# Gram matmuls of a tile in two bursts instead of four groups, and GpSimd's gathers tied more closely to TensorE, in a recommendation tower

## What is computed

```python
e = jnp.stack([tbl_0[ids[:, 0]], ..., tbl_26[ids[:, 26]]], axis=1)   # 2048 x 27 x 128
dot_products = jnp.einsum('bnd,bmd->bnm', e, e)
r, c = np.tril_indices(27, k=-1)
h = jnp.concatenate([dot_products[:, c, r], dense_ctx], axis=1)      # 2048 x 367
h = jnp.maximum(h @ W_top1 + b_top1, 0.0)                            # 512
h = jnp.maximum(h @ W_top2 + b_top2, 0.0)                            # 256
y = h @ W_top3                                                       # 1
```

## Time and profile before

| | us |
|---|---|
| three runs | 361.26, 360.29, 360.21 |
| median | 360.29 |
| profiled execution: span from the first to the last instruction | 358.7 |
| what lies around the span, by the median | 1.6 |
| TensorE busy, matmuls | 333.7 (93%) |
| VectorE busy | 246.3 (69%) |
| ScalarE busy | 144.4 (40%) |
| GpSimd busy | 250.4 (70%) |

### The profile page before, as it was taken

One profiled execution on the slowest core, in us unless ns is written; L12 is line 12 of the kernel. 1 busy time (PEld: TensorE's weight loads), 2 busy tenths in 40 slices (PEclk: granted clock), 3 DMA queues, 4 the chain that ended last, 5 costly groups with the idle time before them and its releaser, 6 DMA issues.

```text
span 358.7 us, 13616 instructions
## 1 busy us (share of the span) xinstructions
PE 333.7 (93%) x6094; PEld 303.4 (85%) x6094; DVE 246.3 (69%) x329; ACT 144.4 (40%) x265; POOL 250.4 (70%) x271
## 2 busy tenths in 40 slices
PE   1879699989999989999999999999999999999896
PEld 0779499978999979898889989999899989997775
DVE  3959979975488935878197965968387955961142
ACT  2536524444433433335343453435343353435320
POOL 5777777777777777777777777777777777777200
PEclk9969989999999999999999999999999999999999
DMA  6997744534333353443333452434533443322100
GB/s 184 306 318 196 205 136 107 102 93 91 83 93 82 90 99 75 96 96 80 93 88 82 115 85 77 105 84 81 102 89 83 99 98 74 84 55 55 27 3 1
DMA packets 26155, 36.86 MB, mean 103 GB/s; under 512 B 8451, under 2 KB 20099, under 8 KB 26098
## 3 DMA queue, kind: packets, MB, share of 16 engines
q0 software_dynamic: 8448, 17.32, 20.5%
q1 hardware_dynamic: 17506, 18.16, 20.1%
q10 hardware_dynamic: 144, 0.52, 0.4%
HBM read 35.97 MB, written 0.01 MB: 100 GB/s over the span
## 4 chain that ended last, share of the span: by engine, by line
PE 57%; POOL 26%; issue 10%; DVE 3%; DMA 3%; ACT 1%; DVEq 0%; ACTq 0%
POOL rows L450 26%; PE e_banks L482 25%; PE w_banks L543 9%; PE g_banks L513 8%; PE w_banks L554 7%; PE e_banks L494 6%; DMA rows<-in_tbl,idx 2%; DVE one_hot L672 2%; PE w_banks L532 1%; DVE zt L686 1%; DMA idx<-in_idx 1%; ACT et L340 0%; ACT h L333 0%; ACT et L350 0%; DVE a L720 0%
## 5 line engine op out<-in xcount | busy, mean ns | idle before, releaser
L450 POOL DMA_INDIRECT rows<-in_tbl,idx x264 | 249.6, 945 | 82.9 <-issue 78.0
L672 DVE TENSOR_TENSOR one_hot<-ids_wide,row_no 128x1024 fp32r<-128x1024 int32 x160 | 186.3, 1215 | 76.5 <-PE e_banks L482 72.5
L482 PE MATMUL e_banks<-one_hot,table_hi 128*128 128x256 f32 x672 | 172.2, 294 | 3.4 <-issue 3.4
L482 PE MATMUL e_banks<-one_hot,table_lo 128*128 128x256 f32 x672 | 167.0, 287 | 0.0
L482 PEld LDWEIGHTS e_banks<-one_hot,table_hi 128*128 128x128 f32 x672 | 131.4, 196 | 4.4 <-issue 4.2
L482 PEld LDWEIGHTS e_banks<-one_hot,table_lo 128*128 128x128 f32 x672 | 131.6, 196 | 0.2
L350 ACT ACTIVATE et<-e_banks 128x256 f32<-128x256 f32 x84 | 57.9, 689 | 89.3 <-PE e_banks L482 89.3
L340 ACT ACTIVATE et<-e_banks 128x512 f32<-128x512 f32 (+1 forms) x68 | 45.0, 664 | 52.3 <-PE e_banks L494 51.5
L513 PEld LDWEIGHTS g_banks<-et 128*26 128x26 f32 x4096 | 41.7, 103 | 17.7 <-issue 13.3
L513 PE MATMUL g_banks<-et 128*26 128x26 f32 x4096 | 50.0, 191 | 1.8 <-DVE zt L686 1.3
L494 PE MATMUL e_banks<-ident,rows 128*128 128x128 f32 x264 | 43.0, 285 | 5.5 <-DMA rows<-in_tbl,idx 5.5
(11 more groups left out here) (25 smaller groups left out, 67.7 us busy)
## 6 DMA issues: line engine op xcount, KB each, us to landing
ids_wide<-in_ids SPq DMA_DIRECT2D x80, 128.0 KB
et<-in_kept_tables SPq DMA_DIRECT2D x10, 512.0 KB, 10.1
rows<-in_tbl,idx POOLq DMA_INDIRECT x264
et<-in_kept_tables ACTq DMA_DIRECT2D x1, 512.0 KB, 3.9
a1T<-in_ids SPq DMA_DIRECT2D x4, 128.0 KB, 10.8
w<-in_w SPq DMA_DIRECT2D x2, 256.0 KB
w<-in_W_top SPq DMA_DIRECT2D x1, 512.0 KB
w<-in_w SPq DMA_DIRECT2D x1, 222.0 KB
```

Of the source, the lines that this page charges most:

```text
L450: pool.indirect_dma_start(rows[:, k % RING, a, :], None, tables[f], bass.IndirectOffsetOnAxis(ap=idx[:, t, f:f + 1], axis=0)).then_inc(row ...
L482: last = nc.tensor.matmul(e_bank[n % E_BANKS][:, 0:UNIT], part[:, q, c, :], one_hot[:, hot_slot(o, piece), c % PIECE, :], start=(c == 0 an ...
L672: nc.vector.tensor_tensor(one_hot[:, hot_slot(o, piece), :, :], ids_place(o).unsqueeze(1).broadcast_to([P, PIECE, UNIT]), row_no[:, piece ...
```

## The change

`BURST_AT` is new: the gram pieces 0 to 3 of a tile stand together at the end of the tile's first tick `at`, pieces 4 to 7 with `turn` and `pack` at the end of tick `at + 2`. `g_filled` is counted up after each burst, so VectorE waits for two. Gram pieces no longer alternate with turns of `h`; look-ups and layers do. The loads by which look-ups are placed are new. GpSimd waits, from chunk 4 on, for the transposes of chunk k - 4 (`AHEAD_BY = 3`), and for every burst that stands in tick k - 4 or earlier.

```diff
+AHEAD_BY = 3
...
+    HALF = G_PIECES // 2
+    BURST_AT = []
     for t in range(LAST_TILE):
         at = TILE_AT[t + 1] + (t == 0)
-        for p in range(G_PIECES):
-            step = [("G", t, p)] + ([("turn", t), ("pack", t)] if p == G_PIECES - 1 else [])
-            grams[at + p * 4 // G_PIECES].append(step)
+        for half, tick in enumerate((at, at + 2)):
+            grams[tick] += [("G", t, p) for p in range(half * HALF, (half + 1) * HALF)]
+            BURST_AT.append(tick)
+        grams[at + 2] += [("turn", t), ("pack", t)]
...
-    COLUMNS = {"T": 1024, "OH": 4096, "G": 1024, "H": 1024, "L1": 3072, "L2": 4096}
-    LOOK_UPS_FROM = [0, TILE_AT[1] + 1] + [TILE_AT[PAIR * (u - 1)] + 4 for u in range(2, UNITS + 1)]
-    load = [sum(COLUMNS[step[0][0]] for step in turns[k] + layers[k] + grams[k]) for k in range(TICKS)]
+    COLUMNS = {"T": 1024, "OH": 4608, "G": 768, "H": 768, "L1": 3072, "L2": 4096}
+    LOOK_UPS_FROM = [0, TILE_AT[1] + 1] + [TILE_AT[PAIR * (u - 1)] + 3 for u in range(2, UNITS)] + [TILE_AT[LAST_TILE]]
+    load = [COLUMNS["T"] + sum(COLUMNS[step[0]] for part in turns[k] + layers[k] + [grams[k][:HALF]] for step in part)
+            for k in range(TICKS)]
...
-        for step in look_ups[k] + layers[k]:
-            STEPS += step
-        for turn, piece in itertools.zip_longest(turns[k], grams[k], fillvalue=[]):
-            STEPS += turn + piece
+        for turn, step in itertools.zip_longest(turns[k], look_ups[k] + layers[k], fillvalue=[]):
+            STEPS += turn + step
+        STEPS += grams[k]
...
-                if k >= RING:
-                    pool.wait_ge(t_filled, k - RING + 1)
+                if k > AHEAD_BY:
+                    pool.wait_ge(t_filled, k - AHEAD_BY)
+                bursts = sum(tick <= k - AHEAD_BY - 1 for tick in BURST_AT)
+                if bursts:
+                    pool.wait_ge(g_filled, bursts)
...
-                if p == G_PIECES - 1:
+                if p % HALF == HALF - 1:
                     last.then_inc(g_filled, 1)
...
-                dve.wait_ge(g_filled, t + 1)
+                dve.wait_ge(g_filled, 2 * (t + 1))
```

## The result

| | before | changed |
|---|---|---|
| median of six runs | 360.45 | 363.93 |
| lowest and highest | 360.2 to 362.13 | 362.61 to 364.92 |
| ratio (95% interval) | | 1.0093 (1.0071 to 1.0114) |
| profiled execution: span | 358.7 | 361.6 (that run: 363.37) |
| TensorE busy | 333.7 | 334.0 |

The forecast was 359.8 us, in 358.7 to 362.0. The time lies outside, on the slow side.

What follows compares the result with a forecast made beforehand. GpSimd's gathers, one per 1.25 us, were taken as the bound. +0.4 at chunk 67's transposes and -0.9 in the tail gave -0.5 us on 360.29: 359.8 us, range 358.7 to 362.0.

Steps and rivals of the forecast that it cites:

- (1): Grams in bursts: each two pairs joined into four pieces save 0.22 us, 6.6 us of TensorE in all, hidden behind gathers.
- TensorE will arrive earlier: At chunks' transposes: TensorE, saved 6.6 us by bursts, reaches chunks that have not landed; only a few tenths gained at chunk 67.
- (3): GpSimd running three chunks ahead: its wait for chunk k-4's transposes bites nowhere, 3 us to spare at chunk 44; cost 0.
- (7): TensorE's clock: gaps of about 2 us before chunks 65 and 66 would not lower it before the tail; taken as 0.
- GpSimd decides at the end: Chunks 24 to 67: gathers need 207.5 us, TensorE 204.5, so GpSimd's 1.25 us cadence sets when the last chunk is in.
- (2): Look-ups placed anew: the same 84, lumps of two per tick covered by GpSimd's cadence; priced at nothing, bound 1.5 us a lump.
- (4): GpSimd's waits for bursts: chunk 10's gather starts 0.3 to 0.6 late, never made up; +0.5 us, bounds 0 and 1.0.
- (5): Tail: tile 14's last grams move ahead of chunk 67's transposes; tile 15's grams start 1.75 us after those, 0.9 less than before.
- (6): Start of chunk 67's transposes: last gather ends at 334.5, 2.0 us of landing, so 336.5 against 336.13, +0.4 us.
- B: Rival: GpSimd's new waits bite more often, as bursts save nothing or look-ups lump; three more stops, 361.3 us; chance 0.08.

Runs made afterwards that it cites:

- e5: The kernel before, gathering only chunks 0 to 6, with later chunks reading those rows again and nothing waiting for gathers: 355.82 us, 0.9878.
- e6: The changed kernel, gathering only chunks 0 to 6, later chunks reading those rows again, without GpSimd's waits: 352.17 us, 0.9794.
- e1: The changed kernel without GpSimd's wait for bursts, its wait for the transposes of chunk k-4 kept: 364.55 us, 1.0101.
- e4: The kernel before in its old order, with GpSimd's new waits for chunk k-4 and for gram groups: 361.89 us, 1.0055.
- e3: The kernel before with only the grams changed: two bursts of four instead of four groups of two, turns of h in a row ahead: 375.46 us, 1.0402.
- e2: The changed kernel with all of GpSimd's waits as before (seven chunks of room, no bursts): 364.74 us, 1.0101.
- e9: The changed kernel with SyncE's plain loads of the same bytes, from fixed places, replacing the gathers of chunks 7 to 67: 354.66 us, 0.9735.
- e10: The changed kernel without the gathers of chunks 7 to 67, plus 250 chained memsets of 128x512 on GpSimd: 352.69 us, 0.9760.
- e11: The changed kernel without GpSimd's wait for bursts, plus 64 tiny matmuls at the start of TensorE's program: 365.76 us, 1.0122.

## Why the prediction was wrong

TensorE's timeline of the kernel before has, right behind the earlier trace rows, a second burst of four gram pieces of tile 15:

```profile
341.88 0.80 PE L513 MATMUL g_banks<-et 128*26 128x26 f32 x72
342.99 0.66 PE L513 MATMUL g_banks<-et 128*26 128x26 f32 x56 [0.31 <-issue]
343.57 1.99 PE L554 MATMUL w_banks<-w,a1T 128*128 128x256 f32 x8
```

The prediction by its own steps:

- **(1), the term that failed.** I took 1.19 for four pieces "since it comes from the only row with four pieces". That row stands in the tail, at 338.76, and GpSimd's last gather starts at 333.08: no gather runs beside it. Beside gathers four pieces take 1.76, with 0.09 on the way in 1.85, against 1.62 for two pairs as they ran on average (0.72 each): 0.23 us lost for each pair joined where 0.22 was to be saved. That is 6.0 for the 26 bursts from T14 to T67, of the 9.6 us that the grams cost more there. Nor was it the only row. The tail of before has a second burst of four pieces, 3 us behind the first, in the rows above: 343.57 - 341.88 = 1.69, with a gap inside and no gather either. The mean of the two, 1.44, and 0.09 on the way in are 1.53 against the 1.50 of two pairs: by both rows the saving was nothing. Without gathers the joined pairs do save, by 3.3 us in the grams themselves (e5 and e6); that T67 is 7.1 sooner there and my sum said 6.6 is luck, since the turns of h and a long gap are in it. The loss beside gathers was outside my bounds, which began at 0 "at least", because I had ruled a loss out with the matmuls being the same. The pairs gave a hint that I did not follow: 10 of 50 took over 0.8 where my row showed 0.66.
- **"TensorE will arrive earlier"**, on which (3) to (7) and the notion that GpSimd decides at the end rested, fell with it. TensorE's busy time was to fall by 6 to 10 us and rose by 0.3; it was 4.2 us later at T67 and bound the kernel. That GpSimd decides at the end did not hold in the kernel before either: its last wait for rows ended at 131.63, and in the earlier trace rows T66 and T67 carry none, so TensorE went without a stop for rows from there on. The two engines stood within 1.5% of each other, as I had worked out; that closeness should have put a large chance on the other one, not only on GpSimd.
- **(2)** right in its price: the look-ups cost 1.98 us each instead of 2.00. That two of them go ahead of T14 moved 4.0 us from one side of T14 to the other.
- **(3)** right in its cost, not in its reason. With `t_filled` alone (e1) GpSimd has 1.9 us of stops, at chunks 42 to 44, where I had 3 us to spare: T40, for which chunk 44 waits, starts at 215.24, a microsecond after the T41 of before. TensorE's lateness had used the margin up, and it also hid the stops.
- **(4)** too small. The stop at chunk 10 is 1.5, above my bound of 1.0, since the gather starts 0.86 behind T7, which stands right behind the burst it waits for, where I had reckoned 0.3 to 0.6. There were five more, 4.9 us in all. "Never made up" was wrong as well: in the changed kernel TensorE's lateness hid them but for 0.57. On before's order the waits alone cost 0.55% (e4).
- **(5)** right: tile 15's grams start 1.65 after T67, forecast 1.75; the steps that lead there are as I had them, ScalarE packing until 341.2 and draining T67 until 341.9. The tail from there to the end is 19.6 against 19.9.
- **(6)** T67 at 336.5 became 340.31, by (1).
- **(7)** right in its result: no fall after 325. The gaps that I argued from never came, since TensorE was late; the one of 1.78 at 331.88 was no wait for rows and did nothing. In e3 the four gaps, of 2.26, 1.65, 1.78 and 2.33 us idle, were each followed by a fall, to 0.62 in the windows above, so "nearer to the 1.50 that did nothing" was no safe ground: 1.65 and 1.78 did it there, and 1.78 here and 2.06 in e6 (before 316.56) did not. The Trainium skill (TensorE: Matmul & The Clock Gate, the part on HAM oscillation) speaks of gaps between bursts that wait for DMA; the falls of e3 agree with the consequence, though no rows were waited for in its gaps.
- **The rivals.** B came nearest: over 1 us of stops on GpSimd, and bursts that save nothing. It had the effect on GpSimd as the price, though; the price was TensorE's own time, and even with its three more stops it came to 361.3, 2.6 short of the time measured. I gave it 0.08.

What stays open: what in an indirect gather holds TensorE. That the pauses come only behind 42 matmuls of a dense group, and that TensorE idles "issue", fits a supply of instructions that is used up faster than it is filled and that a gather interrupts; no run shows the inside of that. How far the spread between runs of e3 and e6 comes from long gaps was not tried.

## What to carry to other kernels

Price an operation by a row in which the other engines do what they will do at its new place, and look for every row that fits: a row from the tail, where the gathers had ended, was out by 0.57 us in 1.19, and its neighbour of the same kind took 1.69. A long run of very small matmuls is not free of its neighbours: split it into groups short enough to slip through, and weigh that against the edge of each group. When two engines stand within a per cent or two of each other, work out the time with each of them as the bound, and take the waits away (as e1 and e2 did) before a stop is blamed.

## What the runs showed of the hardware

- Beside indirect gathers on GpSimd, one in 1.25 us, a run of 128x26 matmuls pauses up to twice per gather, mostly 0.2 to 0.3 us at a time, at fixed points of the gather, from about the 42nd matmul on (50 of 56 pauses in the changed kernel). Without gathers (e6), beside plain loads of the same bytes (e9) and beside memsets of 527 ns (e10) the median burst has none and takes 1.20.
- A gather that waited for a gram burst started 0.86 us behind the start of the transposes that follow the burst, at chunk 10 (53.39 against 52.53) as at chunk 43 (215.20 against 214.34).
- In dense groups of small matmuls TensorE can stand for 1.1 to 2.5 us; the 16 longest gaps all begin beside a packet of the queue that brings instructions. Where such a gap falls depends on the place in the program; 64 matmuls at its start moved one off (e11).
- The clock fell behind gaps of 1.65 to 2.33 us in e3 and stayed at 1.00 behind one of 1.78 in the changed kernel (331.88) and one of 2.06 in e6: the length of a gap alone does not tell.
